# A product-key expert stage without its loop, in another order, with one product moved from VectorE to GpSimd

## The reference

```python
# per token: 8 heads, 64 keys in each of two halves, 64 * 64 = 4096 experts
xn = rmsnorm(x)                                       # x was layer-normed before
q = (xn @ w_q.T).reshape(b, t, H, 2, DK)
sim1 = einsum('bthd,hkd->bthk', q[..., 0, :], keys[:, :, 0, :])
sim2 = einsum('bthd,hkd->bthk', q[..., 1, :], keys[:, :, 1, :])
s1, i1 = top_k(sim1, 8)
s2, i2 = top_k(sim2, 8)
all_idx, all_sc = i1 * 64 + i2, s1 + s2               # 64 pairs per head
fs, pk = top_k(all_sc, 8)
fi = take_along_axis(all_idx, pk)                     # 8 experts per head
hidden = gelu(einsum('btd,bthkd->bthk', xn, expert_down[fi]))
hidden = hidden * relu(fs)
x = x + tanh(g) * einsum('bthk,bthkd->btd', hidden, expert_up[fi])
```

## Time and profile before

| what | us |
|---|---|
| median of three runs (2418.28 to 2422.07) | 2421.75 |
| profiled execution, its own time | 2428.35 |
| its span, first to last instruction | 2426.3 |
| expert stage, from the fold matmuls at 1696.9 to the end | 729.4 |
| one turn inside a pass of the loop, from one first transpose to the next (1968.00 less 1926.43) | 41.57 |
| one turn across the loop's end (2015.06 less 1968.00) | 47.06 |

### The profile page before, as it was taken

One profiled execution on the slowest core, in us unless ns is written; L12 is line 12 of the kernel. 1 busy time (PEld: TensorE's weight loads), 2 busy tenths in 40 slices (PEclk: granted clock), 3 DMA queues, 4 the chain that ended last, 5 costly groups with the idle time before them and its releaser, 6 DMA issues. The chain is left out here.

```text
span 2426.3 us, 46392 instructions
## 1 busy us (share of the span) xinstructions
PE 2217.8 (91%) x18214; PEld 1495.1 (62%) x18244; DVE 1688.9 (70%) x4536; ACT 867.3 (36%) x2003; POOL 118.1 (5%) x128
## 2 busy tenths in 40 slices
PE   7999986989999999997899999998789999999898
PEld 3555543445755746684445555555678788888887
DVE  6788873756556565536777777776778778778685
ACT  5788771240322312204555554544211111111110
POOL 4443101000000000000000000000000000000000
PEclk9999987999999999998999999999999999999999
DMA  5111103000000002001000000000300000000000
GB/s 165 24 36 45 24 7 142 1 1 1 1 1 1 1 0 105 1 1 46 1 1 1 1 1 1 1 1 9 131 1 2 2 11 1 3 11 2 2 10 9
DMA packets 23758, 48.96 MB, mean 20 GB/s; under 512 B 4960, under 2 KB 13408, under 8 KB 22880
## 3 DMA queue, kind: packets, MB, share of 16 engines
q1 hardware_dynamic: 23520, 45.71, 5.6%
HBM read 37.57 MB, written 2.10 MB: 16 GB/s over the span
## 5 line engine op out<-in xcount | busy, mean ns | idle before, releaser
L2021 PEld LDWEIGHTS banks<-work,big 128*128 128x128 f32 x2048 | 254.4, 197 | 10.2 <-issue 1.9
L2021 PE MATMUL banks<-work,big 128*128 128x128 f32 x2048 | 255.7, 280 | 1.9 <-ACT work L2112 1.7
L928 PE MATMUL banks<-big,work 128*128 128x256 f32 x1024 | 241.3, 379 | 3.6 <-issue 3.3
L2128 ACT ACTIVATE work<-banks 128x512 f32<-128x512 f32 x128 | 76.5, 597 | 458.7 <-PE banks L2021 458.7
L854 PE MATMUL banks<-big,work 128*128 128x512 f32 x512 | 221.2, 593 | 0.0
L539 ACT ACTIVATE work<-banks,work 128x512 f32<-128x512 f32 x256 | 173.9, 686 | 122.0 <-DVE work L628 121.9
L928 PEld LDWEIGHTS banks<-big,work 128*128 128x128 f32 x1024 | 195.1, 191 | 33.9 <-issue 1.9
L1689 ACT ACTIVATE work<-work 128x512 f32<-128x512 f32 x256 | 181.0, 711 | 0.0
L854 PEld LDWEIGHTS banks<-big,work 128*128 128x128 f32 x512 | 97.0, 190 | 120.3 <-issue 120.1
L628 DVE TENSOR_REDUCE work<-banks 128x2 f32<-128x1024 f32 x128 | 150.6, 1218 | 14.9 <-PE banks L430 14.9
L2048 PE MATMUL banks<-big,work 128*128 128x256 f32 x512 | 133.5, 409 | 19.2 <-issue 16.9
(11 more groups left out here) (219 smaller groups left out, 3846.9 us busy)
## 6 DMA issues: line engine op xcount, KB each, us to landing
big<-in_bias SPq DMA_DIRECT2D x16, 256.0 KB, 4.2
big<-in_B_val SPq DMA_DIRECT2D x8, 512.0 KB, 6.9
big<-in_B_out SPq DMA_DIRECT2D x1, 4096.0 KB, 19.0
big<-in_D_downT SPq DMA_DIRECT2D x1, 4096.0 KB, 12.6
big<-in_D_up SPq DMA_DIRECT2D x1, 4096.0 KB, 21.9
work<-work SPq DMA_DIRECT2D x120, 32.0 KB, 2.0
big<-big SPq DMA_DIRECT2D x64, 32.0 KB, 2.0
wc<-in_ctxT SPq DMA_DIRECT2D x1, 2048.0 KB, 7.7
```

Source lines behind the costliest of these rows:

```text
L928: last = eng.matmul(XO[qt // 2][:, qt % 2 * D:(qt % 2 + 1) * D], spread[:, c % NG, qt * P:(qt + 1) * P], w_out[:, c, :], start=False, stop ...
L2021: last = eng.matmul(HP[n % 2][:, q * P:(q + 1) * P], down[:, kc * ELO + n * NJ + q, :], xnT[par][:, kc, :], start=(kc == 0), stop=(kc == K ...
```

## The change

Four things are done in one edit.

1. The loop is gone: `turns` calls `turn` for each i, with constants in every wait.
2. TensorE's order. select is split into `turn_x` (the transposes), at the end of slot 3, and `compare` (the similarities), behind spend of slot 4. hidden comes ahead of spend in slot 0. weights comes ahead of hidden in slot 4, and turn_picks ahead of weights in slot 5.
3. VectorE's order. The five parts of topk(i+1) run one slot sooner each: part 0 in slot 5 of the turn before, parts 1 to 4 in slots 0 to 3. onehots(i+1, 0) moves from slot 7 to slot 6, right behind split_score, and onehots(i+1, 1) from the start of the next turn to slot 7.
4. The product `lot` is made by GpSimd, 64 instructions with the operands and shapes that VectorE's had (elo and score parts in, both bf16, 3072 results on each of 128 partitions). weights waits for the new `lot_ready` as well, and split_score waits until the last product of the turn before has read the scores.

```diff
-            turn(0, 0, 2)
-            turn(1, 1, 2)
-            with eng.Fori(0, (NT - 4) // 2) as k:
-                turn(k * 2 + 2, 0, 2)
-                turn(k * 2 + 3, 1, 2)
-            turn(NT - 2, 0, 1)
-            turn(NT - 1, 1, 0)
+            for i in range(NT):
+                turn(i, i % 2, min(2, NT - 1 - i))
...
+                for i in range(NT):
+                    for c in range(NC):
+                        if c == 0:
+                            eng.wait_ge(split.sem, split.at(i, 5))
+                        eng.wait_ge(elo_ready.sem, elo_ready.at(i, c + 1))
+                        free = (i, 2 * c - 2) if c >= 2 else (i - 1, 2 * c + 6)
+                        if w_made.due(*free):
+                            eng.wait_ge(w_made.sem, w_made.at(*free))
+                        halves = [P, CP, 3, NF // 2, 2]
+                        eng.tensor_tensor(lot[c % 2].rearrange("p n f (j two) -> p n f j two", two=2),
+                                          elo[:, c % 2].rearrange("p n (j two) -> p n j two", two=2).unsqueeze(2)
+                                          .to_broadcast(halves),
+                                          scT[:, c * CP:(c + 1) * CP, :, :].unsqueeze(3).to_broadcast(halves), ALU.mult
+                                          ).then_inc(lot_ready.sem, 1)
...
+                def compare(i, par):
+
                     eng.wait_ge(xt_ready.sem, xt_ready.at(i, 1))
+                    if i:
+                        before = (i - 1, SELECT + 1) if i >= 2 else (0, NB)
+                        eng.wait_ge(h_ready.sem, h_ready.at(*before))
...
+                    if i and i < NT - 1 and n in (SELECT + 1, SELECT + 2):
+                        eng.wait_ge(sim_ready.sem, sim_ready.at(i + 1, n - SELECT))
...
                         eng.wait_ge(hot_ready.sem, hot_ready.at(i, n // 2 + 1))
+                        eng.wait_ge(lot_ready.sem, lot_ready.at(i, n // 2 + 1))
...
                     for n in range(NB):
-                        if not first:
+                        if n == 0 and ahead >= 1:
+                            hidden(i + 1, 1 - par, n)
+                        if i:
                             spend(i - 1, 1 - par, n)
-                        if ahead >= 1:
-                            if ahead >= 2 and n == SELECT + 1:
-                                eng.wait_ge(sim_ready.sem, sim_ready.at(i + 2, 2))
+                        if n == SELECT + 1:
+                            if ahead >= 2:
+                                compare(i + 2, par)
+                            weights(i, n)
+                        if n and ahead >= 1:
                             hidden(i + 1, 1 - par, n)
-                        weights(i, n)
-                        if ahead >= 2 and n == SELECT:
-                            eng.wait_ge(h_ready.sem, h_ready.at(i + 1, n + 1))
-                            select(i + 2, par)
-                        if ahead >= 1 and n == PICK:
+                        if n == PICK and ahead >= 1:
                             turn_picks(i + 1)
+                        if n != SELECT + 1:
+                            weights(i, n)
+                        if n == SELECT and ahead >= 2:
+                            turn_x(i + 2)
...
                 def split_score(i):
 
+                    if i:
+                        eng.wait_ge(lot_ready.sem, lot_ready.at(i - 1, NC))
...
-                                      ALU.is_equal)
-                    eng.wait_ge(elo_ready.sem, elo_ready.at(i, c + 1))
-                    halves = [P, CP, 3, NF // 2, 2]
-                    eng.tensor_tensor(lot[b].rearrange("p n f (j two) -> p n f j two", two=2),
-                                      elo[:, b].rearrange("p n (j two) -> p n j two", two=2).unsqueeze(2).to_broadcast(halves),
-                                      scT[:, at, :, :].unsqueeze(3).to_broadcast(halves), ALU.mult
-                                      ).then_inc(hot_ready.sem, 1)
+                                      ALU.is_equal).then_inc(hot_ready.sem, 1)
...
                 def turn(i, par, ahead):
-                    onehots(i, 1)
                     for n in range(NB):
                         apply(i, par, n)
                         if n in (1, 3):
                             onehots(i, 2 + n // 2)
-                        if n == 2 and (not isinstance(i, int) or i >= 2):
+                        if n == 2 and i >= 2:
                             update(i - 2, par)
-                        if ahead >= 1 and n < 5:
-                            topk(i + 1, n)
+                        if ahead >= 1 and n < 4:
+                            topk(i + 1, n + 1)
+                        if ahead >= 2 and n == PICK:
+                            topk(i + 2, 0)
                         if ahead >= 1 and n == PICK + 1:
                             split_score(i + 1)
+                            onehots(i + 1, 0)
                         if ahead >= 1 and n == NB - 1:
-                            onehots(i + 1, 0)
+                            onehots(i + 1, 1)
```

More of the change, by code:

```diff
@@ L1936, in product_key_experts @@
         h_made, h_ready = sig("hidden_made", ELO // NJ), sig("hidden_ready", ELO // NJ)
-        elo_ready, hot_ready = sig("elo_ready", NC), sig("hot_ready", NC)
+        elo_ready, hot_ready, lot_ready = sig("elo_ready", NC), sig("hot_ready", NC), sig("lot_ready", NC)
         w_made, g_ready = sig("weights_made", NB), sig("weighted", NB)
@@ L1940, in product_key_experts, with turns @@
         norm = Norm(nc, ctx, m, "D", take, 1e-6, NT)
-        def turns(eng, turn):
-            turn(0, 0, 2)
-            turn(1, 1, 2)
-            with eng.Fori(0, (NT - 4) // 2) as k:
-                turn(k * 2 + 2, 0, 2)
-                turn(k * 2 + 3, 1, 2)
-            turn(NT - 2, 0, 1)
-            turn(NT - 1, 1, 0)
+        def turns(turn):
+            for i in range(NT):
+                turn(i, i % 2, min(2, NT - 1 - i))
         with nc.Block() as block:
@@ L2065, in turn @@
                 def turn(i, par, ahead):
-                    first = isinstance(i, int) and i == 0
                     for n in range(NB):
-                        if not first:
+                        if n == 0 and ahead >= 1:
+                            hidden(i + 1, 1 - par, n)
+                        if i:
                             spend(i - 1, 1 - par, n)
-                        if ahead >= 1:
-                            if ahead >= 2 and n == SELECT + 1:
-                                eng.wait_ge(sim_ready.sem, sim_ready.at(i + 2, 2))
-                            hidden(i + 1, 1 - par, n)
-                        weights(i, n)
-                        if ahead >= 2 and n == SELECT:
-                            eng.wait_ge(h_ready.sem, h_ready.at(i + 1, n + 1))
-                            select(i + 2, par)
-                        if ahead >= 1 and n == PICK:
-                            turn_picks(i + 1)
-                turns(eng, turn)
+                        if n == SELECT + 1:
[3 more added lines that the diff above has]
+                        if n and ahead >= 1:
+                            hidden(i + 1, 1 - par, n)
+                        if n == PICK and ahead >= 1:
+                            turn_picks(i + 1)
+                        if n != SELECT + 1:
+                            weights(i, n)
+                        if n == SELECT and ahead >= 2:
+                            turn_x(i + 2)
+                turns(turn)
                 for n in range(NB):
@@ L2097, in stage @@
                         eng.wait_ge(xt_made.sem, xt_made.at(i - 1, 1))
[L2098 to L2100 removed]
+                    eng.activation(xstage, x[:, i, :],
+                                   ACT.Identity, scale=norm.rstd[:, i:i + 1],
+                                   bias=norm.shift[:, i:i + 1]).then_inc(staged.sem, 1)
                 def select(i, par):
@@ L2286, in update @@
                     eng.wait_ge(up_made.sem, up_made.at(i, 1))
-                    xt = x[:, i, :] if isinstance(i, int) else x[:, bass.ds(i, 1), :].rearrange("p a d -> p (a d)")
+                    xt = x[:, i, :]
                     eng.scalar_tensor_tensor(out=xt, in0=UPP[par][:, 0:D], scalar=gate, in1=xt, op0=ALU.mult, op1=ALU.add
@@ L2294, in _ @@
                 onehots(0, 0)
+                onehots(0, 1)
+                topk(1, 0)
                 def turn(i, par, ahead):
-                    onehots(i, 1)
                     for n in range(NB):
```

11 lines of the change are left out of this document (6 added, 5 removed).

## The result

| | before | after |
|---|---|---|
| median of the timed runs | 2420.0 us (2409.9 to 2422.1) | 2498.0 us (2497.6 to 2499.1) |
| profiled execution, its span | 2426.3 us | 2496.4 us |
| time after / before | | 1.032, 95% interval 1.030 to 1.035 |
| expert stage (1716 us to the end): TensorE, VectorE, GpSimd busy | 642, 534, 0 us | 655, 658, 400 us |

A forecast was written before the change was run, and what follows sets the result against it. TensorE was taken to set the pace. With VectorE held out by GpSimd's products, the expert stage would gain 126.5 us and turn 0 15, together 141 on the 2421.75 us median: 2563 us, range 2385 to 2605.

The forecast's parts named there:

- The loop: Expert stage: TensorE's standing and slow clock at the hardware loop's five returns vanish when turns are written out, saving 24.6 us.
- The three waits: TensorE's waits for ScalarE's copy, topk's last step and the last apply get covered, 2.3 to 2.5 us a turn.
- The mechanism: GpSimd's product keeps VectorE's steps with two SBUF inputs out for up to 6.7 us; TensorE then waits for the picks.
- the blocked turn: Expert-stage turn with VectorE's two-operand steps held behind four GpSimd products: 51.7 us a turn, 2563 us total, chance 0.58.
- shared: Rival: VectorE's two-operand steps only stretch beside GpSimd's products; 41.0 us a turn, 2395 us, chance 0.24.
- short products: Rival: a GpSimd product takes 5.0 us or less, down to 3.4; 39.1 us a turn, 2356 us, chance 0.10.
- the change doesn't do what it says: Rival: the written-out expert stage still stands for its instructions, so the returns' 24.6 us stay; given no time of its own.
- the length of a product: One GpSimd product of 3072 elements takes 6.7 us, from 2.12 ns an element and 0.19 fixed; lower bound 3.4.
- The wait ahead of weights 0: TensorE waits for a turn's first GpSimd product ahead of weights 0, 2 to 3 us a turn.
- The wait ahead of the picks: TensorE stands idle 8 to 10 us a turn ahead of the picks, since topk's last part ends late.
- the signs that the prediction named: Profile signs of blocking, including GpSimd's product group near 6.7 us mean and TensorE's clock under 0.9 in every turn.
- The stated point of decision: GpSimd product length at which the held-up turn equals the old mean of 43.4 us: 4.6 us; under it, not slower.

The follow-up runs named there:

- run 2: The kernel before with all turns written out instead of the hardware loop, nothing else; 2398.3 us, 0.989 of before.
- run 1: The changed kernel with the 64 products made by VectorE again and lot_ready gone, written-out loop and new orders kept; 2358.7 us, 0.973 of before.
- run 4: The changed kernel with hot ahead of elo in onehots, so VectorE is done with both when GpSimd's product may begin; 2488.2 us, 1.028 of before.
- runs 1 to 3 and 5 to 8: All eight follow-up kernels except the changed kernel with hot ahead of elo; measured from 2358.7 to 2480.7 us.
- run 5: The changed kernel with VectorE's part of topk ahead of onehots in slots 1 and 3, products still on GpSimd; 2380.7 us, 0.983 of before.
- run 7: The changed kernel with topk back in the slots of the kernel before, products still on GpSimd; 2458.8 us, 1.016 of before.
- run 3: The changed kernel with each GpSimd product replaced by two fills that read nothing from SBUF, expert sum left out; 2365.1 us, 0.976 of before.

## Why the prediction was right, and where it was off

*The loop:* forecast 24.6, measured 24 (run 2). *The three waits:* forecast 39.1 us a turn with nothing else changed, measured 39.05 (run 1). Over the stage the prediction gave some 33 us for them, and the new order took 40. Two readings in these terms are loose, without weight for the result: from transposes to similarities the row has 2016.20 - 2015.06 = 1.14, not 1.37, and 1820.26 - 1778.84 is 41.42, where the 498.7 for twelve turns goes by the 41.57 of a turn in a pass. *The mechanism:* the held steps, their order and the wait for the picks came as the blocked turn had them, save that hot was never held (1.22 at most); it held GpSimd off instead. The rivals fell: "shared" by the durations above, "short products" by 5.34 against its bound of 5.0 and the held steps, "the change doesn't do what it says" by run 2.

*The size:* the term that failed is the length of a product. I took 6.7 us, from the line through GpSimd's two f32 rows, between bounds of 3.4 and 6.7, so the value was the upper bound. It is 5.34 (run 4): less the same fixed 0.19, 1.68 ns an element, a fifth less than the 2.12 of the f32 rows. The product differs from these rows in its shapes and repeated operands as well as in its type, so how much of the fifth is the type's is not shown. The blocked turn, by ends of products, forecast against measured:

| interval | forecast | measured |
|---|---|---|
| product 0 to 1 | 8.5 | 6.88 |
| product 1 to 2 | 8.4 | 6.89 |
| product 2 to 3 | 14.1 | 12.65 |
| product 3 to picks | 4.2 | 4.17 |
| picks to the next product 0 | 16.0 | 17.19 |
| turn | 51.7 (51.2 and what clock was added) | 47.78 |

Each interval but the fourth holds one product, 1.36 us shorter than I took it; elo, of which only 0.55 is left when a product ends, gives the last 0.2 of the first two. The fifth also holds the slow clock, which I had added behind the sum: 16.0 - 1.4 + 2.5 = 17.1. The wait ahead of weights 0 was given as 2 to 3 and is 1.22, since that product too is 1.4 shorter. The wait ahead of the picks was given as 8 to 10 and is 5.26: the three products between are 4.6 shorter with the steps behind them (8.5 + 8.4 + 14.1 against 26.4), while TensorE is there 25.3 behind the end of product 0, 0.7 sooner than the 26 that I took. Two of the signs that the prediction named came out weaker than stated: the group of the product has a mean of 6.25, not near 6.7, and the clock in a turn is 0.93, not under 0.9.

The account closes. From the first weights of turn 1 to those of turn 15 the changed kernel takes 2454.55 - 1787.03 = 667.5 us, 47.7 a turn, where I had 723.8: 56 too much. Turn 15 to the last up matmuls takes 24.8 for 29.6, its three products in line being short as well: 5 too much. For turn 0 I had 15 more than before. The two executions reach it at different times, here by the first elo of before, to set beside the row of L2281 above:

```profile
L2259 DVE TENSOR_TENSOR wc<-work,wc x64: 678/685/693, 1739.3 to 2399.6; 128x1024 bf16<-128x1024 bf16 x64
```

The 5.2 us by which the changed kernel is ahead there lie in code that the change doesn't touch; in runs 1 to 3 and 5 to 8 that first elo starts at 1730.9 to 1738.9. Counted from the first elo, the first weights come at 7.2 instead of 3.6, and turn 0 takes 45.8 us instead of 39.6, together 9.8 more, 5 less than I had. The picks of the next tile, in before and after:

```profile
1769.52 0.91 PE L2009 MATMUL banks<-ident,work 128*64 128x64 f32 x12 [7.04 <-DVE work L2236]
```

```profile
1771.37 0.91 PE L2022 MATMUL banks<-ident,work 128*64 128x64 f32 x12 [10.07 <-DVE work L2256]
```

The kernel before already stood 7.04 us there, and the blocked chain took part of that wait's place. So 56 + 5 + 5 = 66 of the forecast 141 are too much, 75 are left, and the medians differ by 78.

The stated point of decision, 4.6 us for a product, can't be read off as it stands. With 5.34 the same sum gives the turn 4 x (5.34 - 4.6) = 3.0 above the old mean of 43.4, 46.4, and 47.7 was measured. It was a fair guide, but run 5 shows that no length by itself decides: with the same products the kernel is 42 us faster than before if other steps stand behind the one-hots. That the time fell inside the range owes something to the range, which took in the shared case too, from 2385 on.

## What to carry to other kernels

Before work that reads SBUF goes to GpSimd, look at what stands in VectorE's queue behind the instruction that releases it. Each such GpSimd instruction can hold one VectorE step for its whole length, so put PSUM operands, max and max_index there, keep SBUF-to-SBUF steps that lead to the next matmul ahead of the release, and don't expect much from splitting the GpSimd instruction (17 us of 139 here). Small casts and tensor_scalars with one operand can be held too, so they don't belong behind it either. VectorE wasn't the pace here, and relieving it bought nothing: the new order and the unrolled loop alone gave 64 us, and the best kernel with the products on GpSimd (2380.7) was slower than run 1 without them (2358.7).

## What the runs showed of the hardware that I had not expected

- Small steps with one operand are held too: a 128x64 uint32 tensor_scalar took 3.64 us for 0.19 (run 7), a 128x128 cast from uint32 to bf16 4.22 for 0.21 (run 4).
- The hold goes both ways and is counted in an instruction's own duration, on both engines: no idle time shows it, and GpSimd's record has 6.25 us where the same product takes 5.34 with no two-operand step running ahead of it (run 4).
- A fill on GpSimd takes 0.86 ns an element (3.10 us for 3600) and leaves two-operand steps on VectorE undisturbed, at 0.68 us, while a 128x64 f32 tensor_scalar with one operand took 1.60 for 0.20 beside it (run 3).
- A wait of 5.26 us on TensorE cost 2.5 us more behind it, about the 2.6 that the rows of before had given for one of 4.55.
